# Message stages of a graph network: every row added on VectorE, and one float32 selection product in place of two rounded ones

## The reference

```python
def _gine_layer(x, src, dst, edge_attr, eps, We, be, W1, b1, ...):
    e = edge_attr @ We + be                       # 5000 edges x 512
    m = jax.nn.relu(x[src] + e)                   # messages
    agg = jax.ops.segment_sum(m, dst, num_segments=x.shape[0])
    h = ((1.0 + eps) * x + agg) @ W1 + b1
    ...
x = x + _L1_gnn_ref(_layernorm(x, axis=-1), edge_index, edge_weight1, ...)
```

## Time and profile before

| what | us |
|---|---|
| median of three runs | 4565.56 (4561.38 to 4593.44) |
| profiled execution, its own time | 4567.96 |
| profiled execution, span of the core | 4566.2 |
| message stages, first gather of each to first gather of the hidden stage behind it | 103.36, 98.76, 91.60, 94.48 |

### The profile page before, as it was taken

The page is one execution under the profiler, slowest core; times in us unless marked ns, Lnnn a source line. Parts: engine busy times, 40 slices in busy tenths (PEclk is TensorE's granted clock), DMA queues, the critical chain, the costliest instruction groups (busy, mean ns, idle before and its releaser), DMA issues. The chain is left out here.

```text
span 4566.2 us, 65043 instructions
## 1 busy us (share of the span) xinstructions
PE 4090.5 (90%) x22652; PEld 3320.6 (73%) x22652; DVE 2797.6 (61%) x5416; ACT 2084.9 (46%) x3584; POOL 1496.6 (33%) x1431
## 2 busy tenths in 40 slices
PE   7888999889977878689999899998899998999967
PEld 3447788777766656449988589886699874998844
DVE  5665666569965667468844455443555434557888
ACT  1223233333357333265567433575434764335566
POOL 1442266228821758654400323101332003330010
PEclk9988999999988588799999899999999998999965
DMA  8985488449965869764423655224643237544677
GB/s 308 401 325 179 164 289 264 173 154 378 390 213 165 289 146 176 155 221 154 156 75 116 194 178 163 95 101 157 217 156 114 93 124 235 162 147 142 184 197 211
DMA packets 462790, 886.22 MB, mean 194 GB/s; under 512 B 73189, under 2 KB 113750, under 8 KB 461711
## 3 DMA queue, kind: packets, MB, share of 16 engines
q1 hardware_dynamic: 297611, 525.71, 33.7%
q0 software_dynamic: 90016, 237.51, 18.8%
q10 hardware_dynamic: 74872, 119.23, 7.4%
HBM read 609.61 MB, written 303.62 MB: 200 GB/s over the span
## 5 line engine op out<-in xcount | busy, mean ns | idle before, releaser
L2076 POOL DMA_INDIRECT hidden_agg<-edge_sums,edge_where x316 | 353.5, 1119 | 700.5 <-DVE layer_raw_inner L2163 287.5
L1921 POOL DMA_INDIRECT message_x<-g,edge_partner x120 | 119.2, 993 | 782.0 <-POOLq L150 458.2
L783 PE MATMUL hidden_O<-hidden_xh,layer_hi_inner 128*128 128x256 f32 (+1 forms) x1280 | 367.6, 287 | 0.0
L785 PE MATMUL hidden_O<-hidden_xl,layer_hi_inner 128*128 128x256 f32 (+1 forms) x1280 | 361.5, 282 | 0.0
L784 PE MATMUL hidden_O<-hidden_xh,layer_lo_inner 128*128 128x256 f32 (+1 forms) x1280 | 360.8, 282 | 0.0
L2120 ACT ACTIVATE hT_inner<-hidden_O,hidden_b 128x256 f32<-128x256 f32 (+1 forms) x320 | 124.1, 471 | 333.9 <-PE hidden_O L785 333.9
L783 PE MATMUL root_O<-root_hi,root_xh 128*128 128x512 f32 (+1 forms) x632 | 254.0, 402 | 14.0 <-DVE root_xl L1183 14.0
L783 PE MATMUL output_O<-layer_hi_inner,output_hh 128*128 128x512 f32 (+1 forms) x632 | 250.2, 396 | 1.7 <-DVE output_hl L2257 1.7
L785 PE MATMUL output_O<-layer_lo_inner,output_hh 128*128 128x512 f32 (+1 forms) x632 | 249.7, 395 | 0.0
L784 PE MATMUL output_O<-layer_hi_inner,output_hl 128*128 128x512 f32 (+1 forms) x632 | 249.6, 395 | 0.0
L2266 DVE TENSOR_TENSOR layer_raw_inner<-output_O,output_b2t 128x1024 f32<-128x1024 f32 x80 | 96.9, 1211 | 246.3 <-PE output_O L785 246.3
(11 more groups left out here) (499 smaller groups left out, 12580.2 us busy)
## 6 DMA issues: line engine op xcount, KB each, us to landing
edge_sums<-message_res SPq DMA_DIRECT2D x160, 256.0 KB
layer_raw_inner<-g SPq DMA_DIRECT2D x78, 512.0 KB, 4.1
g<-layer_raw_inner SPq DMA_DIRECT2D x78, 512.0 KB
room<-in_L_gnn_basis SPq DMA_DIRECT2D x30, 1280.0 KB, 13.8
order_basis<-in_L_gnn_basis SPq DMA_DIRECT2D x18, 1280.0 KB, 14.3
edge_sums<-relation_res SPq DMA_DIRECT2D x82, 256.0 KB
order_x<-in_x SPq DMA_DIRECT2D x39, 512.0 KB
normed<-order_y ACTq DMA_DIRECT2D x39, 512.0 KB
```

The lines of the kernel that those rows point to most:

```text
L783: eng.matmul(out, a_hi, b_hi, start=start, stop=False)
L785: return eng.matmul(out, a_hi, b_lo, start=False, stop=stop)
L1921: eng.indirect_dma_start(x[t % R][:, :], None, table, bass.IndirectOffsetOnAxis(ap=ed.partner[1][:, t:t + 1], axis=0)).then_inc(ga[t % R], 16)
L2076: eng.indirect_dma_start(agg[j % R][0:n, :], None, ed.sums[1], bass.IndirectOffsetOnAxis(ap=ed.where[1][0:n, c:c + 1], axis=0)).then_inc(g ...
```

## The change

All in the message stages.

- **Sum.** `attr` makes only the edge term, in one product. VectorE adds x to it for every tile (`total`) into z, now a ring of 4. In the first layer the same instruction multiplies x by its row's rstd, and the shift is left to the ReLU's bias; `norm` on ScalarE is gone.
- **ReLU and selection.** ScalarE writes one float32 m (ring of 10). mh, ml, `high` and `low` are gone. `sums` is one float32 product with a float32 select, and lags 3 tiles behind `attr` where it lagged 2.
- **Rings.** x and res have 10 buffers each. The border copy is issued before the store. `result` lags 2 tiles. The last ten tiles count on semaphores of their own: TensorE's merge waits for the last ten border copies, SyncE for the last ten stores at the end.
- **Weights.** In the ahead stages W1 is loaded before all else, and both halves of the split stand in front of the first tile. In the first layer the load comes after store(12), the split's high part behind result(18), the low part in tile 20's batch. The row loads for the next stage come after store(24).
- **Powers.** In the first layer statistics are taken in batches (of 1, 1 and 2 tiles, then nine of 4): one variance, one power and one shift for each batch.
- **Idle products** are 14 in front and 20 behind the first four `attr` in the first layer, and 14 behind them in the others (34 and 18 before, all in front).

```diff
-    W, R, XR = 4, 8, 4
+    R, XR, ZR, MR, W = MESSAGE_ROWS, 4, 4, 4, 10
...
+                if ahead:
+                    split.load(eng)
...
                 def store(t):
-                    if t == 2:
+                    main, border = (st[t % W], st[t % W]) if t < ET - W else (s["tail"], s["edge"])
+                    eng.wait_ge(s["res"], t + 1)
+                    eng.dma_start(borders[t:LAST + t + 1:LAST, :], res[t % W][0:P:P - 1, :]).then_inc(border, 16)
+                    eng.dma_start(ed.sums[1][t * P:(t + 1) * P, :], res[t % W][:, :]).then_inc(main, 16)
+                    if t == WEIGHT_AT and not ahead:
                         split.load(eng)
-                    eng.wait_ge(s["res"], t + 1)
-                    eng.dma_start(ed.sums[1][t * P:(t + 1) * P, :], res[t % W][:, :]).then_inc(st[t % W], 16)
-                    eng.dma_start(borders[t:LAST + t + 1:LAST, :], res[t % W][0:P:P - 1, :]).then_inc(st[t % W], 16)
+                    if t == ROWS_AT:
+                        eng.wait_ge(s["wlo"], 1)
+                        for g in range(2):
+                            eng.dma_start(raw[:, g * TILES:(g + 1) * TILES, :], rows(table, g, False)).then_inc(s["xin"], 16)
...
                 def gather(t):
-                    if t >= R:
-                        wait_sum(eng, t - R)
+                    wait(eng, s["z"], t - R + 1)
...
+                static_pipeline([(0, gather)] + ([(LOOK, batch_ended)] if normal else []), ET)
...
+                def total(t):
                     eng.wait_ge(ga[t % R], (t // R + 1) * 16)
-                    eng.wait_ge(s["E"], of_dve(t))
-                    wait(eng, s["mh"], t - W + 1)
-                    wait(eng, s["ml"], t - W + 1)
-                    eng.tensor_tensor(sum_of(t)[:, :], X[t % XR][:, :], x[t % R][:, :], ALU.add).then_inc(s["z"], 1)
...
+                    eng.wait_ge(s["E"], t + 1)
+                    wait(eng, s["m"], t - ZR + 1)
+                    if normal:
+                        eng.scalar_tensor_tensor(z[t % ZR][:, :], x[t % R][:, :], rs[:, t:t + 1], X[t % XR][:, :],
+                                                 ALU.mult, ALU.add).then_inc(s["z"], 1)
+                    else:
+                        eng.tensor_tensor(z[t % ZR][:, :], X[t % XR][:, :], x[t % R][:, :], ALU.add).then_inc(s["z"], 1)
...
                 if normal:
-                    static_pipeline([(0, stats), (1, shift), (3, low)], ET)
+                    for b in range(len(batches) + 1):
+                        fresh = batches[b] if b < len(batches) else range(0)
+                        ready = batches[b - 1] if b else range(0)
+                        for k in range(max(len(fresh), len(ready))):
+                            if k < len(fresh):
+                                stats(fresh[k])
+                            if k == 0 and b:
+                                shift(b - 1)
+                            if k < len(ready):
+                                total(ready[k])
+                        if b < len(batches):
+                            variance(b)
+                        if WEIGHT_AT + 8 in ready:
+                            split.low(eng)
+                else:
                     split.low(eng)
-                else:
-                    static_pipeline([(0, add), (1, low), (1, weight_low)], ET)
+                    static_pipeline([(0, total)], ET)
...
+                def message(t):
+                    eng.wait_ge(s["z"], t + 1)
+                    wait(eng, s["B"], t - MR + 1)
...
+                        eng.activation(m[t % MR][:, :], z[t % ZR][:, :], ACT.Relu).then_inc(s["m"], 1)
...
                 def sums(t):
...
-                    eng.wait_ge(s["ml"], t + 1)
+                    eng.wait_ge(s["m"], t + 1)
                     wait(eng, s["res"], t - 2)
-                    eng.matmul(B[t % 3][:, :], select[:, t, :], mh[q][:, :], start=True, stop=False)
-                    eng.matmul(B[t % 3][:, :], select[:, t, :], ml[q][:, :], start=False, stop=True).then_inc(s["B"], 1)
...
+                    eng.matmul(B[t % 3][:, :], select[:, t, :], m[t % MR][:, :], start=True, stop=True).then_inc(s["B"], 1)
...
-                for q in range(W):
-                    eng.wait_ge(st[q], 32 * (ET // W))
+                eng.wait_ge(s["edge"], 16 * W)
```

116 lines of the change are left out of this document (44 added, 72 removed).

## The result

The kernel after takes 4625.95 us (median of 4, 4618.65 to 4627.7), beside 4572.38 for the kernel before in the same set of runs. The ratio is 1.012, 95% interval 1.0094 to 1.0145: 1.2% slower, where the prediction had 4498 and faster. The profiled execution has a span of 4616.9 us at a mean granted clock of 0.888 (0.911 before).

The account below looks back on a forecast made before the run. TensorE was taken as the bound with DMA close behind, plus a stall and low clock after it; 57 us saved in three ahead stages and 10 in the first: 4568 - 67 - 2.4, about 4498, range 4464 to 4538.

Parts of the forecast that it names:

- TensorE starts and stays at the low clock: Rival for all message stages: 2.44 us a tile at 1.20 GHz, 85 us slower, 4651 in total; chance 0.07.
- The step that failed: Start of an ahead stage: TensorE idles some 4 us, may begin at low clock for a few tiles; 2 us.
- The first stage: First message stage: VectorE bounds it at 1.73 us a tile; saves about 10 us, bounds 0 and 16.
- TensorE per tile: Ahead stages: attr 0.36 and one float32 product 0.86 make 1.22 us, where it was 1.505.
- DMA per tile: Ahead stages: gather, store and borders, 0.528 MB, take 1.38 us and set the pace; bounds 1.25 and 1.57.
- The rival of 1.57: Rival: DMA sets 1.57 us a tile, three stages 7.4 later each, the first 2; 4522 in total; chance 0.20.
- GpSimd per tile: Ahead stages: a gather and its gap take 1.25 us, no gather long any more; bounds 1.25 and 1.50.
- The stall: Ahead stages: the result copy's 7 us wait goes, since ten result buffers cover about 14 us of store time.
- The sum: Ahead stages 76 us each, saving 57 us; with 10 from the first stage 67 us, total about 4498; chance 0.66.

Follow-up runs that it names:

- kernel 7: The kernel after with only TensorE's order changed from attr, sum, attr, sum to attr, attr, sum, sum; 4499.44 us, ratio 0.9854.
- kernel 11: The kernel after with three idle products of 128 rows behind every selection sum in all four message stages; 4623.41 us, ratio 1.0126.
- kernel 12: The kernel after with three idle products of 5 rows behind every selection sum in all four message stages; 4890.32 us, ratio 1.0714.
- kernel 16: The same kernel as kernel 7, measured again beside its variants in a later set of runs; 4497.44 us, ratio 0.9859.
- kernel 2: The kernel after with 34 idle products instead of 14 in the later stages and 56 instead of 20 in the first; 4524.17 us, ratio 0.9897.
- kernel 17: Kernel 7 with four result buffers in place of ten, measured in the same set as kernel 16; 4532.33 us, ratio 0.9931.
- kernel 3: The kernel before with ten result buffers instead of four and nothing else of the change; 4535.13 us, ratio 0.9922.
- kernel 5: The kernel after with each sum as two fp32r products on a rounded m, low part left out; 4565.45 us, ratio 0.9959.
- kernel 6: Kernel 2 with TensorE's order changed to attr, attr, sum, sum; 4552.38 us, ratio 0.9934.
- kernel 14: Kernel 7 with the first layer's powers and variances by single tiles instead of fours; 4558.24 us, ratio 0.9938, beside a before of 4585.

## Why the prediction was wrong, step by step

**The forecast against the rivals.** "TensorE starts and stays at the low clock", with "an ahead stage 10 + 40 x 2.44 + 11 = 119, the first about 117", is what happened in three stages of four: 123.9, 120.8 and 121.7. It had a chance of 0.07. Its bound "decides where the clock is low in more than about half of a stage's tiles" was right as well, and its price was short by 0.28 us a tile (2.72). Its reason was not right: it had gaps of 0.2 to 0.5 us in every tile, and at the low clock TensorE has none (10.00 busy of 10). So the rival named the outcome and not how it comes about.

**The step that failed** is in the start of an ahead stage: TensorE "may begin at the low clock: 2.44 a tile instead of 1.22 for a few tiles ... I put 2 us". The gap was forecast (some 4 us; 4.02 measured), and so was the low clock. "For a few tiles" was wrong. The argument against the rival was that "at the low clock TensorE has no gaps at all, and the third stage's clock came back after the stall". No gaps is right, 10.00 busy of 10, and does not suffice. The clock came back in the kernel before with other neighbours: in every second tile an identity product of 128 rows stood between attr and the two sums. I took the recovery over to a mix in which a 5-row attr follows every single sum, without asking whether the mix had a part in it. By the Trainium skill, TensorE: Matmul & The Clock Gate, section "What's actually happening", being busy is what releases the low clock. In the rows here that is so where products of 128 rows stand together (kernels 7 and 11), and not of every engine that the profile calls busy all the time: 10.00 of 10 us at 0.50 in the kernel after, and in kernel 12 the clock even falls out of such a stretch.

**The first stage**: "VectorE is" the bound, 1.73 a tile, saves 10 us. With the order of pairs it measured 91 to 93 (kernels 16 and 7), near the forecast 93. That is in part luck: the clock was low for some of it (0.78 over the stage in kernel 7), which the forecast didn't have. VectorE's batch takes 6.57 us there (shifts at 1961.55 and 1968.12 of kernel 16), 1.64 a tile, and its wait for the power is 0.34 to 0.35, where I had 6.9 and 0.5. What I left out are TensorE's gaps in this stage. Two of 1.63 and 1.90 us come at its start with the first batches, and one comes in mid-stage, where ScalarE waits for W1 and splits it (2.87 us in kernel 2). I had counted that split only on VectorE.

**TensorE per tile**, "0.36 and 0.86 make 1.22", was 1.48 in the order attr, sum. The 0.86 was read from float32 products back to back; beside an attr the start-to-start time is 1.06, and the attr's 0.42. In pairs a pair costs 2.57 us (2578.38 to 2580.95 in kernel 7), 1.29 a tile. Two tiles cost 2.96 with four changes between the two kinds of product and 2.57 with two, so a change costs about 0.2 us here. I could have seen it: 1.505 was fitted as a sum of prices in which the changes were already mixed.

**DMA per tile**, 1.38 taken between 1.28 and 1.57: at 404 to 408 GB/s the 0.528 MB are 1.30 us. The low end was right, and the deep rings do run it there (third stage, DMA share 1.04 at 404 GB/s). The rival of 1.57 is refuted, and with it, over 35 us on end in kernel 7 (2575 to 2610, six of the seven five-us slices at 400 GB/s and more, the first at 377), the 358 GB/s of the Trainium skill, DMA: Bandwidth & Descriptors, section "Where 436 GB/s comes from", as a bound of this path with one core at work.

**GpSimd per tile**, 1.25: right. Gathers all take 0.94 or 0.95 in mid-stage; the only long one of a stage (2.44 us at 2578.00 in the second) lies beside the split's low part, which reads two tensors in SBUF. That is what the rule of the Trainium skill, SBUF — State Buffer, section "SBUF: two separate sides", gives.

**The stall** goes, right: the ring is worth 35 us by kernels 16 and 17, and 34 by kernel 3 (4535 against 4569).

**The sum.** With the order of pairs, in which the clock comes back after a few tiles as the sum assumed, the stages are 91.2, 77.1, 75.2 and 74.9 against the forecast 93, 76, 76, 76, and the total 4497 to 4499 against 4498. So close a match is in part luck. The pace was 1.29 a tile where the sum had 1.38, and in kernel 7's second stage it was TensorE's (busy 5.00 of 5 us from 2560 to 2610), not the feed's. The end was slower. From the end of the last border copy's issue to the next stage's gather it is 2623.40 - 2612.98 = 10.4 us in kernel 7, where the earlier trace rows gave 7.8, since SyncE, at some 1.1 us a tile, runs behind at the end and the last border copies meet ten stores in flight: the merge waits 6.36 us for them. The kernel after's own third stage, 76.6 us, is luck of the same kind: TensorE set 1.48 a tile there, from a first sum 10.7 us into the stage. So the forecast's 76 was about right for a stage whose clock comes back, by terms that erred against each other, and the order attr, sum does not bring that case.

## What to carry to other kernels

When a change alters which products TensorE alternates between, ask of the kernel before not only whether the low clock came back after a stall, but under which products, and whether the new mix keeps those; "busy" in the profile doesn't answer it. Where small products of few rows must run beside large ones, put them in pairs or larger runs, so that the large ones stand together: here that alone took the ratio from 1.012 to 0.985, saved two changes of kind in every pair of tiles, and made late rows cost microseconds instead of a stage. And price a product from a row in which its neighbours are those of the new kernel.

## What the runs showed of the hardware that I had not expected

- TensorE stayed at 1.2 GHz for over 100 us while the profile has it busy all the time, with 128-row float32 sums and 5-row fp32r products in turn (second and fourth stages of the kernel after). It did so with two fp32r sums between attr products too (kernel 5, second stage, 69 us with one gap of 0.48 us).
- With three more 5-row products a tile it even fell from 2.4 to 1.2 GHz without a gap before it (kernel 12, third stage, at 3340).
- The same products in the order attr, attr, sum, sum brought 2.4 GHz back within about 8 us of the first sum (kernel 7, second stage), 14 us of a gap (kernel 6, second stage) and 16 us of one (kernel 7, first stage). So did three idle products of 128 rows behind each sum (kernel 11), and three of 5 rows did not (kernel 12). By what the chip counts, rows or something that goes with them, these runs don't say; an attr of 128 rows was not tried.
- The DMA engines moved 400 to 411 GB/s with gathers from memory and stores to it mixed, for 30 us on end (kernel 7, 2580 to 2610).
- Conditions moved a later stage of the same code between 74 and 91 us from one set of runs to another (kernels 7 and 14), with waits for transfers of up to 7.2 us in the longer ones; why the transfers come late is open. The kernel with ten result buffers and pairs is the fastest here, 4497 us.
